# Layer 1's softmax sums taken from a column of ones in the output product

## What is computed

```python
# layer 1, xn = layernorm(x)
scores = jnp.einsum('bqd,bkd->bqk', q, k) * scale
attn = jax.nn.softmax(scores, axis=-1)
s = jnp.einsum('bqk,bkd->bqd', attn, v)
...
# f: 8 experts, the best 2 of each token weighted by their gates
hmid = jax.nn.gelu(jnp.einsum('th,eih->tei', x, w_fc), approximate=False)
y = jnp.einsum('tei,ehi->teh', hmid, w_proj)
out = jnp.einsum('teh,te->th', y, gates)
```

## Time and profile before

| what | us |
|---|---|
| median of 3 runs | 712.23 |
| lowest and highest | 711.32, 712.45 |
| the profiled execution, its own time | 712.29 |
| span of its profile | 710.5 |
| TensorE busy | 404.0 |
| VectorE busy | 324.1 |
| GpSimd busy | 269.1 |
| ScalarE busy | 259.3 |

### The profile page before, as it was taken

How to read it: one execution, slowest core, us unless ns; L and a number is a source line. 1 busy time by engine, 2 the same in 40 slices (tenths; PEclk the granted TensorE clock), 3 DMA queues, 4 the chain that set the end, 5 groups by cost and what they waited for, 6 DMA issues and landing times. The chain is left out here.

```text
span 710.5 us, 8856 instructions
## 1 busy us (share of the span) xinstructions
PE 404.0 (57%) x2582; PEld 364.4 (51%) x2582; DVE 324.1 (46%) x1167; ACT 259.3 (36%) x505; POOL 269.1 (38%) x324
## 2 busy tenths in 40 slices
PE   0873020676332019999512929299721674897996
PEld 0752020565321019999512919298610563786885
DVE  7871200486740015765000415068600491988853
ACT  1410000241000006767201515166411372886985
POOL 7467775001777730000474262500577166000000
PEclk9977555688655559999865968689955697998999
DMA  7999212000112114552521524242211011000000
GB/s 187 362 278 403 71 52 74 30 0 9 48 63 68 52 44 134 168 170 95 168 62 52 175 78 134 74 134 90 64 52 53 19 54 51 16 16 15 10 23 24
DMA packets 45903, 65.17 MB, mean 92 GB/s; under 512 B 8586, under 2 KB 23331, under 8 KB 45859
## 3 DMA queue, kind: packets, MB, share of 16 engines
q1 hardware_dynamic: 37666, 47.83, 21.1%
q0 software_dynamic: 8192, 16.79, 7.8%
HBM read 28.93 MB, written 35.65 MB: 91 GB/s over the span
## 5 line engine op out<-in xcount | busy, mean ns | idle before, releaser
L549 POOL DMA_INDIRECT slot_rows<-xn_tok,slot_of x128 | 125.6, 981 | 104.9 <-DVE slot_of L1270 66.4
L563 POOL DMA_INDIRECT onehot<-expert_rows,slot_of x64 | 61.8, 966 | 185.0 <-DMA expert_rows<-zeros 131.5
L1404 DVE TENSOR_TENSOR act<-sg,ps 128x384 f32<-128x384 f32 x48 | 26.6, 554 | 161.2 <-issue 101.0
L563 POOL DMA_INDIRECT route_tmp<-expert_rows,slot_of x64 | 60.7, 948 | 36.2 <-issue 19.0
L743 PE MATMUL ps<-w_gu,raw_fc 128*128 x192 | 41.0, 363 | 41.8 <-ACT raw_fc L1000 38.7
L734 PE MATMUL ps<-w_dn,actT 96*128 x384 | 54.0, 286 | 18.3 <-issue 15.9
L1006 ACT ACTIVATE sg<-ps 128x384 f32<-128x384 f32 x48 | 23.5, 491 | 106.8 <-remote 67.7
L661 PE MATMUL ps<-shd,hs_h 128*128 128x128 f32 x128 | 21.5, 321 | 70.1 <-issue 40.1
L734 PEld LDWEIGHTS ps<-w_dn,actT 96*128 96x128 f32 x384 | 49.2, 201 | 19.7 <-issue 19.6
L743 PE MATMUL ps<-w_gu,raw_pr 128*128 x192 | 40.2, 358 | 31.9 <-issue 31.7
L661 PEld LDWEIGHTS ps<-shd,hs_h 128*128 128x128 f32 x128 | 19.7, 228 | 73.8 <-issue 41.3
(11 more groups left out here) (242 smaller groups left out, 919.2 us busy)
## 6 DMA issues: line engine op xcount, KB each, us to landing
slot_rows<-zeros SPq DMA_DIRECT2D x12, 1024.0 KB, 9.7
rows<-slot_rows SPq DMA_DIRECT2D x48, 256.0 KB
expert_rows<-zeros SPq DMA_DIRECT2D x48, 256.0 KB, 2.0
x_tok<-in_L_attn_x_dram SPq DMA_DIRECT2D x8, 256.0 KB, 4.9
slot_rows<-xn_tok,slot_of POOLq DMA_INDIRECT x128
out_dram<-raw_fc SPq DMA_DIRECT2D x16, 128.0 KB
w_dn<-in_L_ffn_w_down_dram SPq DMA_DIRECT2D x1, 1536.0 KB
onehot<-expert_rows,slot_of POOLq DMA_INDIRECT x64
```

What stands on the lines that cost most here:

```text
L549: g.indirect_dma_start(out=slot_rows[r], out_offset=bass.IndirectOffsetOnAxis(ap=slot_of[:, n:n + 1], axis=0), in_=xn_tok[:, r * HT + t, : ...
L563: g.indirect_dma_start(out=gath[b % 4][:, j, :], out_offset=None, in_=expert_rows[r], in_offset=bass.IndirectOffsetOnAxis(ap=slot_of[:, n: ...
L1404: v.tensor_tensor(act[u][:].rearrange("p (a b) i -> p a b i", a=2), sg[u][:].rearrange("p (a b) i -> p a b i", a=2), ps[:, 1 + 2 * u:3 + 2 ...
```

## The change

The values get a column of ones at column 128, and the bias moves to column 129 (`VW = P + 2`). The output product takes 129 columns in place of 128 for each half of the queries, so that its last column is the sum of that row's exponentials. The exponentials on ScalarE no longer write an accumulator, and the tile `den` is gone. The reciprocal on VectorE reads the two sums from PSUM bank 2, with a step of 129 columns. Since it needs the output product it waits for `d_o` in place of `d_p`, and it stands behind `gate_hidden` in place of ahead of it. In the first layer, where the weights are prepared, two copies on ScalarE become four, and VectorE sets two columns with a memset before it splits the biases. The rest of the kernel is as it was.

```diff
--- before.py
+++ after.py
@@ -36,7 +36,7 @@
 ST = -(-(HT * P * TOP0 + E0 * (P - 1)) // P // GT) * GT
 SG = ST // GT
 FSEQ = NSEQ // 2
-VW = P + 1
+VW = P + 2
 
 
 NORM_AT = {-1: 3, 3: 4, 5: 5, 8: 6, 10: 7}
@@ -165,7 +165,7 @@
         raw_fc = sb("raw_fc", [P, CH1, P])
         raw_pr = sb("raw_pr", [P, E1, I1])
         raw_g1 = sb("raw_g1", [E1, P])
-        w1T = sb("w1T", [P, 2 * P + 2])
+        w1T = sb("w1T", [P, 2 * P + 3])
         fcT = sb("fcT", [P, CH1, P])
         prT = sb("prT", [P, CH1, P])
         g1T = sb("g1T", [P, E1])
@@ -261,7 +261,6 @@
         gT = [logits[:].rearrange("p t e -> p (t e)").bitcast(BF16)[:, u * BT * P:(u + 1) * BT * P]
               for u in range(2)]
         nmx = sb("nmx", [P, 2])
-        den = sb("den", [P, 2])
         rden = sb("rden", [P, 2])
         pr = hs_h[1]
         pT = hs_t[1]
@@ -891,8 +890,8 @@
                 pe.wait_ge(d_pTs, b + 1)
                 for j in range(2):
                     for k in range(2):
-                        mm = pe.matmul(ps[:, 2, j * P:(j + 1) * P], pT[:, k, j * P:(j + 1) * P],
-                                       v_sb[u][:, k, 0:P], start=(k == 0), stop=(k == 1))
+                        mm = pe.matmul(ps[:, 2, j * (P + 1):(j + 1) * (P + 1)], pT[:, k, j * P:(j + 1) * P],
+                                       v_sb[u][:, k, 0:P + 1], start=(k == 0), stop=(k == 1))
                 mm.then_inc(d_o, 1)
 
 
@@ -965,11 +964,13 @@
             copy_half(0)
             exp_top(0)
             sc.wait_ge(wT_ps, 4)
-            a.copy(w1T[:], bank(2, 2 * P + 2)).then_inc(wT_sb, 1)
+            a.copy(w1T[:, 0:2 * P], bank(2, 2 * P))
+            a.copy(w1T[:, 2 * P + 1:2 * P + 3], ps[:, 2, 2 * P:2 * P + 2]).then_inc(wT_sb, 1)
             a.copy(fcT[:].rearrange("p a b -> p (a b)"), bank(3)).then_inc(wT_sb, 1)
             a.copy(prT[:].rearrange("p a b -> p (a b)"), bank(4)).then_inc(wT_sb, 1)
             a.copy(g1T[:], bank(5, E1))
-            a.copy(bv_all, ps[0:3, 5, P:P + VW]).then_inc(wT_sb, 1)
+            a.copy(bv_all[:, 0:P], ps[0:3, 5, P:2 * P])
+            a.copy(bv_all[:, P + 1:VW], ps[0:3, 5, 2 * P:2 * P + 1]).then_inc(wT_sb, 1)
 
 
             def stage_s(it, u):
@@ -1106,7 +1107,7 @@
                 if b >= 2:
                     sc.wait_ge(d_fin, b - 1)
                 for j in range(2):
-                    last = a.activation(o_sb[u][:, j, :], ps[:, 2, j * P:(j + 1) * P], ACT.Copy,
+                    last = a.activation(o_sb[u][:, j, :], ps[:, 2, j * (P + 1):j * (P + 1) + P], ACT.Copy,
                                         scale=rden[:, j:j + 1])
                 last.then_inc(d_os, 1)
 
@@ -1117,7 +1118,7 @@
                 sc.wait_ge(d_qk, b + 1)
                 if b:
                     sc.wait_ge(d_s, b)
-                a.activation(key_of, ps[:, 6, 0:SEQ], ACT.Identity, bias=w1T[:, 2 * P + 1:2 * P + 2],
+                a.activation(key_of, ps[:, 6, 0:SEQ], ACT.Identity, bias=w1T[:, 2 * P + 2:2 * P + 3],
                              scale=-SCALE).then_inc(d_qks, 1)
 
             def keep_values(b, u):
@@ -1133,7 +1134,7 @@
                 sc.wait_ge(d_nmx, b + 1)
                 for j in range(2):
                     last = a.activation(pr[:, j, :], pr[:, j, :], ACT.Exp,
-                                        bias=nmx[:, j:j + 1], scale=-1.0, accum_out=den[:, j:j + 1])
+                                        bias=nmx[:, j:j + 1], scale=-1.0)
                 last.then_inc(d_p, 1)
                 batch, place = batch_of(b)
                 if place == 0:
@@ -1347,9 +1348,12 @@
             def split_biases():
 
                 dve.wait_ge(wT_sb, 4)
-                v.tensor_scalar(w1T[:, 2 * P:2 * P + 2], w1T[:, 2 * P:2 * P + 2], -SCALE, None,
+
+                v.memset(w1T[:, 2 * P:2 * P + 1], 0.0)
+                v.memset(bv_all[:, P:P + 1], 1.0)
+                v.tensor_scalar(w1T[:, 2 * P + 1:2 * P + 3], w1T[:, 2 * P + 1:2 * P + 3], -SCALE, None,
                                 ALU.mult).then_inc(biases, 1)
-                link(v.tensor_scalar(bv_all[:, P:VW], bv_all[:, P:VW], -SCALE, None, ALU.mult))
+                link(v.tensor_scalar(bv_all[:, P + 1:VW], bv_all[:, P + 1:VW], -SCALE, None, ALU.mult))
                 with nc.allow_low_precision("three bfloat16 parts hold a float32 exactly"):
                     link(v.tensor_copy(bv_parts[:, 0, :], bv_all))
                     link(v.tensor_tensor(bv_rest, bv_all, bv_parts[:, 0, :], ALU.subtract))
@@ -1555,7 +1559,7 @@
                 dve.wait_ge(d_s, b + 1)
                 dve.wait_ge(d_vs, b + 1)
                 for j in range(2):
-                    last = v.tensor_scalar(pr[:, j, :], ps[:, 6, j * SEQ:(j + 1) * SEQ], v_sb[u][:, j, P:VW], None,
+                    last = v.tensor_scalar(pr[:, j, :], ps[:, 6, j * SEQ:(j + 1) * SEQ], v_sb[u][:, j, P + 1:VW], None,
                                            ALU.add, ALU.min, accum_out=nmx[:, j:j + 1])
                 last.then_inc(d_nmx, 1)
 
@@ -1574,11 +1578,11 @@
                     rstd1(summed(b))
                 elif summed(b) is not None:
                     sum_experts(summed(b))
-                dve.wait_ge(d_p, b + 1)
+                gate_hidden(b, u)
+                dve.wait_ge(d_o, b + 1)
                 if b:
                     dve.wait_ge(d_os, b)
-                v.reciprocal(rden[:], den[:]).then_inc(d_rden, 1)
-                gate_hidden(b, u)
+                v.reciprocal(rden[:], ps[:, 2, 0:2 * (P + 1)].rearrange("p (j n) -> p j n", j=2)[:, :, P]).then_inc(d_rden, 1)
                 if b + 1 < NSEQ:
                     least(b + 1, 1 - u)
                 if b and gated(b - 1) is not None:
```

## The result

| | kernel before | changed kernel |
|---|---|---|
| median of 7 runs, us | 711.83 | 718.40 |
| lowest and highest | 710.09, 712.45 | 714.89, 721.55 |
| the profiled execution, its own time | 712.29 | 718.40 |
| span of its profile | 710.5 | 716.7 |

The changed kernel is slower: the ratio of after to before is 1.0088, with a 95% interval from 1.0070 to 1.0107; by the medians it is 6.6 us. The forecast was 719.2 us in a range from 714.6 to 723.0.

What follows compares the result with a forecast made beforehand. No engine alone was taken to bound the kernel: TensorE, ScalarE and VectorE hold each other, with little slack between VectorE and TensorE. 5.7 + 1.0 + 0.15 = 6.9 us on 712.29 gave 719.2 us, range 714.6 to 723.0.

Steps and rivals of the forecast that it cites:

- the main term: VectorE's queue in layer 1: waiting for the output product delays `least`, gates, `finish` and so the expert sums, 5.7 us.
- the gathers' stretch: Batches 0 to 4, while GpSimd gathers: later `least(2)` delays the sum of experts releasing GpSimd; 1.0 us, ends 0 and 1.65.
- plain batch: Batches 12 and 14: product to expert sums takes at least 2.37 us; loses 0.36 us in batch 12, 0.66 in 14.
- batches 9 to 10: `least(10)` begins 1.14 us later, and VectorE has no real pause until `finish(9)`, so `expert_sum(10)` is that much later.
- Batches 7 to 8: `least(8)` begins 0.70 us later, and all of it arrives at the `finish` for which TensorE waits.
- the rival of one more fall of the clock: New waits bring TensorE's lower clock to another batch: 1.7 to about 3 us more, 721 to 723 us; chance 0.16.
- The prediction's last rival: While GpSimd gathers, shifted work meets the engines' unexplained standstills otherwise: some 2 us up or down; no chance of its own.
- The odd column: TensorE's output matmuls with 129 columns cost 0.11 us a batch over nine batches: 1.0 us, range 0 to 2.0.
- The third of the cases named: The 0.055 us read behind the values' 129-column matmuls belongs to the change of weights, so nothing changes.
- the longer way: ScalarE's scaled copies start 0.25 us behind the product instead of 0.10: 0.15 more a batch, against 0.18 saved on readouts.
- The reciprocal out of PSUM: VectorE's reciprocal reading PSUM: the skill implied 0.06 us more each, 0.6 over ten batches; left out of the sum.
- layer 0 (the preparation): Two more ScalarE copies and two VectorE memsets in the first layer cost 0.15 us, range 0 to 0.3.

Runs made afterwards that it cites:

- wait_only: Kernel before with the reciprocal behind `gate_hidden` and waiting for the output product, sums still from the accumulator: 471.16 us against 465.51, ratio 1.0121; repeat 470.90 against 465.20.
- least_first: Changed kernel with `least(b+1)` moved ahead of VectorE's wait for the output product: 713.74 us against 713.42 for the kernel before, ratio 1.0005.
- order_only: Kernel before with `gate_hidden` ahead of the reciprocal, which still waits for the exponentials: 466.72 us against 465.51, ratio 1.0021.
- column_only: Kernel before with the ones column, wider product and preparation, but accumulator sums and VectorE's order as before: 465.37 us against 465.51, ratio 1.0000.
- after_again: Changed kernel unaltered, run again on a chip of the first, slower kind: 717.51 us against 713.42 for the kernel before, ratio 1.0061.
- no_readout: Kernel before without the accumulator's sums, `den` being a constant, waits and order as before: 464.72 us against 465.51, ratio 0.9980.
- after_third: Changed kernel unaltered, run once more on a chip of the faster kind: 469.45 us, ratio 1.0104 to the kernel before.
- copies_late: `least_first` with ScalarE's scaled copies of batch b-1 behind the exponentials of batch b: 465.95 us against 465.07 for the kernel before, ratio 1.0003.

## Why the prediction was right

**The mechanism.** VectorE's wait ahead of `least` was named as the main term, 5.7 us. `wait_only` measured order and wait together: +5.7 us, twice. `least_first` took only the wait's place away, and the loss went. That the two numbers are equal is in part chance. The 5.7 of `wait_only` has the order's 1 us in it, and the forecast's 5.7 has 1.0 for the gathers' stretch, in which `wait_only` loses little (41.7 us from `output(0)` to `expert_sum(4)`, against 41.0 in `order_only` and 41.9 in `column_only`).

**Its pieces.** Against the table of lateness by batch in the first section: plain batch 12 forecast 0.36, measured 0.44; batch 14 0.66 and 0.73; batch 11 with gates 0.92 and 0.94; batches 6 and 13 together 0.9, measured 0.24 + 0.40 = 0.64; batches 9 to 10 1.14, measured 0.32 + 1.15 = 1.47. The least gap of a plain batch came out as 0.15 + 2.16 + 0.14 = 2.45 us where the sum had 0.12 + 2.15 + 0.10 = 2.37. That is the 0.08 by which batches 12 and 14 are over. Readings of the earlier trace rows were worth what they said. One sentence of the prediction isn't right, and nothing hung on it: batches don't all take 7.8 us or more. The output products of batches 13 and 15 began 7.68 and 7.03 us behind the one before.

**Batches 7 to 8.** Forecast 0.70; measured 1.84 + 0.55 = 2.39. The traces tell them apart. `least(8)` began 0.47 us behind the product's start before, and 1.20 behind it after:

```profile
625.51 2.59 PE L819 MATMUL ps<-prT,rows 128*128 128x128 f32 x16 [1.40 <-DVE raw_fc L1554]
631.42 1.05 PE L893 MATMUL ps<-w_gu,hs_t 128*128 128x129 f32 x8
...
632.62 0.48 DVE L1562 TENSOR_SCALAR_CACHE_REDUCE hs_h<-ps,w_gu 128x256 f32<-128x256 f32 x1
```

So 0.73 is the wait. The other 1.64 came ahead of it: `expert_sum(6)` began at 625.51 in both traces, and the product of batch 7 at 629.78 before and 631.42 after. In between TensorE was busy in both. The windows (stretch, length, busy us of PE, PEld, DVE, ACT, POOL, granted clock, DMA, GB/s) show the clock, before and after:

```profile
625.50:629.80 4.30, 4.29 (x35) 4.13 (x36) 2.94 (x10) 3.26 (x7) 0.00 (x0) 1.00 0.10 30
```
```profile
625.50:631.40 5.90, 5.89 (x34) 5.57 (x35) 2.81 (x9) 3.02 (x7) 0.00 (x0) 0.71 0.07 22
```

It was at its upper level before, 2.4 GHz, and for part of the stretch at the lower one after; ahead of it TensorE had waited 1.40 us for `finish`, where it had waited 1.16 before. This is the rival of one more fall of the clock. It occurred beside the forecast, with 1.6 us of the 1.7 to 3 that it was given. Whether the change brings it is open. `after_again` shows it at the same place (`expert_sum(6)` takes 2.56 us), and the kernel before and `least_first` don't (2.03 and 2.02). But of the two executions with the wait alone one shows it (2.51) and the other doesn't (2.02), though TensorE waited 1.5 us there in both; and `no_readout`, which has no new wait, shows it too (2.85) and is faster all the same.

**The gathers' stretch.** Forecast 1.0, with ends 0 and 1.65; measured +4.32 to `expert_sum(4)`, of which batch 5 gives 1.39 back, so 2.9. The step that failed is that term's size. The mechanism is there: from `output(0)` to the gather that GpSimd starts behind the sum of experts it was 567.93 - 510.88 = 57.05 us, and is 58.60:

```profile
559.39 0.48 DVE L1562 TENSOR_SCALAR_CACHE_REDUCE hs_h<-ps,w_gu 128x256 f32<-128x256 f32 x1
...
566.31 0.95 POOL L562 DMA_INDIRECT onehot<-expert_rows,slot_of  x1 [16.79 <-DVE trig L1424]
```

That is 1.55 us, and 2.0 in the second pair of executions (56.41 and 58.44), where I had put 1.65 at the upper end: nothing of it was taken up. Of the rest, 2.7 us lie between that gather and `output(4)`, 32.16 us before and 34.86 after, and only 0.1 from there to `expert_sum(4)`. The hidden products of batch 5 ran in 3.50 us at a lower clock where they took 2.53, but this hardly counts: the projection behind them had waited 0.68 us for VectorE's minima before, and now it doesn't wait. Between the gather and `output(4)` engines stand still for long in both kernels, VectorE for 14.78 us in one go before and 15.58 after, by the profile for "remote". I can't assign the 2.7 us.

One such standstill falls on the new wait itself. In batch 0 the product is done at 508.87, and the reciprocal that waits for it starts 5.06 us later:

```profile
507.71 1.16 PE L893 MATMUL ps<-w_gu,hs_t 128*128 128x129 f32 x8
...
513.93 0.17 DVE L1585 RECIPROCAL rden<-ps 128x2 f32<-128x2 f32 x1 [5.71 <-remote]
```

In `after_again` it is 5.09, in `after_third`, on the other kind of chip, 0.03. It is not seen further on: from `output(0)` to `output(1)` it is 49.45 us, and was 49.88. The prediction's last rival, that shifted work meets the standstills otherwise and is some 2 us up or down, thus occurred beside the forecast.

On the chips without long standstills the stretch shows no cost: `output(0)` to `expert_sum(4)` is 41.4 us in the changed kernel, 41.9 in `column_only` and 41.0 in `order_only`.

**The odd column.** Forecast 1.0 us; it is 0. The step that failed is the reading of 0.28 us behind the second values' matmul as the price of a column. The values now have 130 columns, an even number, and the same place still leaves 0.28:

```profile
670.95 0.44 PE L853 MATMUL ps<-w1T,xn_tok 128*128 128x130 f32 x2
671.23 0.60 PE L878 MATMUL ps<-ident,hs_h 128*128 128x128 f32 x4
```

while eight passes of 129 columns take the same 1.05 us as eight of 128. So it doesn't come from the width. The third of the cases named, that it belongs to the change of weights behind the values, is what is left; no run shows it by itself. The Trainium skill ("TensorE: Matmul & The Clock Gate", Back-to-back issue gap) made the 129th column worth 0.4 ns, in its formula for a matmul by itself; the 278 and 279 ns of the two groups agree with it.

**ScalarE.** Forecast: readouts -0.18 and the longer way +0.15 a batch, nothing in sum. The readouts' price on the engine was read rightly: in batch 12, from the first exponential to the keys behind the second, it was 682.63 - 681.63 = 1.00 us and is 687.40 - 686.59 = 0.81. Of that, -0.8 us in all reached the kernel's time, where 2.7 were the most. The longer way is 0.15 us in fact (copies 0.25 behind the product, before 0.10) and costs nothing, as `least_first` and `copies_late` show. So this term was -0.8 to -1.4, not 0. The step that failed is that the longer way was set against the readouts: it costs nothing, and they gain a little.

**The reciprocal out of PSUM.** It took 169 ns on average against 162. The Trainium skill ("VectorE: DVE Perf Modes", The TRN2 errata) would have made it 0.06 us longer; the trace shows 0.007. Leaving it out of the sum was right.

**The sum.** Split at the starts of `output(0)` and `expert_sum(4)`, with what batch 5 gives back counted to the gathers' stretch:

| part | forecast | measured in the spans |
|---|---|---|
| layer 0 (the preparation) | +0.15 | -3.17 |
| the gathers' stretch | +1.0 | +2.93 |
| the rest of layer 1: wait 4.7, column 1.0 | +5.7 | +6.44 |
| sum | +6.9 | +6.2 |

The forecast missed the time by 0.8 us, better than its terms. In the rest of layer 1 the column (1.0 too high) and the readouts' small gain stand against the clock (1.6), which was not in the sum. The gathers' stretch came out 1.9 too long, and a layer 0 that was 3.2 us shorter in this execution, which is no effect of the change, covered it. That the total fell on 718.4 owes something to luck. The repeats show it: by the medians the changed kernel was 6.6 us slower here, but 4.1 (`after_again`, 2.9 to 5.9 by its interval) and 4.3 (`after_third`, 3.6 to 6.0) elsewhere, and the forecast's 6.9 lies above both intervals. The wait was right in kind and, where the clock stayed out of it, in size to within 0.4 us a batch or pair of batches.

## What to carry to other kernels

An operand that comes for nothing from one engine is not free if the instruction that reads it must stand in a queue until the product is done: count what stands behind that instruction, here `least`, the gates and `finish`, and who waits for the last of it. Move such a wait behind work that doesn't need it; here one move gave back the loss, to within 0.3% of the time. Readouts on an engine that waits each batch anyway are worth a fraction of their busy time, here some 0.8 of 6.0 us, so there was little to win from the start.

## What was not expected of the hardware

The same program takes 718 us on one chip and 469 on others, though both run layer 1's later part alike. The groups of the first 300 us, with GpSimd's gathers and ScalarE's copies of layer 0, in the changed kernel on the slower chip,

```profile
L548 POOL DMA_INDIRECT slot_rows<-xn_tok,slot_of x128 | 126.8, 991 | 104.5 <-DVE slot_of L1271 66.1 <-issue 38.4
...
L980 ACT ACTIVATE hs_t<-ps 128x512 f32<-128x512 f32 x16 | 9.4, 597 | 118.0 <-remote 81.8 <-PE ps L650 36.2
```

and on the faster:

```profile
L548 POOL DMA_INDIRECT slot_rows<-xn_tok,slot_of x128 | 130.3, 1018 | 50.8 <-issue 38.7 <-DVE slot_of L1271 12.1
...
L980 ACT ACTIVATE hs_t<-ps 128x512 f32<-128x512 f32 x16 | 9.6, 597 | 45.4 <-PE ps L650 45.4
```

The work itself is as long (597 ns a copy, 991 and 1018 ns a gather). The idle time differs: 81.8 us ahead of ScalarE's copies that the profile puts down to "remote" are missing on the faster chip. `output(0)` begins at 508 us on the one and at 318 on the other, and from `expert_sum(4)` to `expert_sum(15)` it is 103 and 104 us. What the engines stand still for was not found. Kernels that differ by a few us must therefore be timed beside each other on one chip.
